# ScalarE works in pairs of steps in the hyperbolic attention loop

## The reference, cut to what matters

```python
q = split_heads(x @ Wq.T); k = split_heads(x @ Wk.T); v = split_heads(x @ Wv.T)
diff_sq = jnp.maximum(q_norm_sq + k_norm_sq - 2.0 * qk, 0.0)
denom = jnp.maximum((1.0 - CURV * q_norm_sq) * (1.0 - CURV * k_norm_sq), 1e-06)
cosh_arg = jnp.maximum(1.0 + 2.0 * CURV * diff_sq / denom, 1.0)
distance = jnp.where(cosh_arg > 1.0, jnp.arccosh(jnp.maximum(cosh_arg, 1.0 + 1e-12)), 0.0)
attn = jax.nn.softmax(-distance, axis=-1)
out = jnp.einsum('bhnm,bhmd->bhnd', attn, v)
```

## Time and profile before

| What | Value |
|---|---|
| median of the runs | 1381.49 us (1377.48 to 1388.93) |
| profiled execution, its own time | 1367.83 us |
| span of that execution | 1365.8 us |
| mean granted TensorE clock | 0.71 of full speed |
| TensorE busy | 974.9 us, 71% |
| VectorE busy | 962.9 us, 71% |
| ScalarE busy | 762.0 us, 56% |
| GpSimd busy | 492.1 us, 36% |

### The profile page before, as it was taken

How to read it: one execution, slowest core, us unless ns; L and a number is a source line. 1 busy time by engine, 2 the same in 40 slices (tenths; PEclk the granted TensorE clock), 3 DMA queues, 4 the chain that set the end, 5 groups by cost and what they waited for, 6 DMA issues and landing times. The chain is left out here.

```text
span 1365.8 us, 17519 instructions
## 1 busy us (share of the span) xinstructions
PE 974.9 (71%) x5593; PEld 495.0 (36%) x5593; DVE 962.9 (71%) x2073; ACT 762.0 (56%) x986; POOL 492.1 (36%) x294
## 2 busy tenths in 40 slices
PE   5887822589999637999364678887787889164385
PEld 2553221256666436998120001111111112034384
DVE  6676598368888263555678999999999999236511
ACT  4204513226666603443243599999999999931031
POOL 0000000200000005664145686888678786200075
PEclk9997965659999957999575555555555555655588
DMA  4001000213110006663234100100010000020064
GB/s 145 0 0 28 0 0 19 68 38 98 42 35 25 9 32 201 214 210 128 75 93 135 44 23 27 41 25 23 24 36 34 24 23 0 0 64 5 36 185 138
DMA packets 59289, 80.25 MB, mean 59 GB/s; under 512 B 13185, under 2 KB 36540, under 8 KB 58944
## 3 DMA queue, kind: packets, MB, share of 16 engines
q1 hardware_dynamic: 50208, 67.33, 15.5%
q0 software_dynamic: 3968, 8.13, 2.0%
q10 hardware_dynamic: 5024, 3.67, 0.8%
HBM read 63.56 MB, written 15.34 MB: 58 GB/s over the span
## 5 line engine op out<-in xcount | busy, mean ns | idle before, releaser
L2483 POOL TENSOR_TENSOR hb_t<-hb_t,hb_r 128x1024 f32<-128x1024 f32 x124 | 330.0, 2699 | 110.1 <-ACT hb_r L2301 110.1
L2238 PE MATMUL hb_psR<-ha_q,ha_k 20*128 20x512 bf16 x256 | 126.3, 592 | 59.8 <-DVE hb_dpos L2495 59.4
L2495 DVE TENSOR_SCALAR hb_dpos<-hb_psR 128x1024 f32<-128x1024 f32 x128 | 155.6, 1217 | 18.9 <-PE hb_psR L2229 10.1
L2503 DVE SCALAR_TENSOR_TENSOR hb_t<-hb_psR,hb_dpos 128x1024 f32<-128x1024 f32 x128 | 155.1, 1212 | 0.0
L2250 PE MATMUL hb_psO<-hb_t,ha_va 128*9 128x512 f32 x512 | 111.5, 969 | 56.2 <-ACT hb_t L2324 56.2
L1843 ACT ACTIVATE ga_att<-ga_psB 128x512 f32<-128x512 f32 (+3 forms) x256 | 102.1, 453 | 74.5 <-PE ga_psB L1775 69.8
L1864 DVE TENSOR_REDUCE ga_nm<-ga_psA 128x1 f32<-128x128 f32 (+3 forms) x256 | 114.3, 485 | 36.0 <-PE ga_psA L1751 32.5
L2229 PE MATMUL hb_psR<-ha_q,ha_k 78*128 78x512 bf16 x256 | 126.2, 595 | 10.0 <-DVE hb_t L2503 3.0
L2512 DVE SCALAR_TENSOR_TENSOR hb_r<-hb_t 128x1024 f32<-128x1024 f32 x64 | 124.5, 1946 | 0.0
L2324 ACT ACTIVATE hb_t<-hb_t 128x4096 f32<-128x4096 f32 x32 | 113.8, 3602 | 0.0
L1625 POOL MEMSET ga_q<- 64x8192 bf16 x1 | 6.9, 6920 | 248.5 <-POOLq L1552 248.5
(11 more groups left out here) (469 smaller groups left out, 2213.5 us busy)
## 6 DMA issues: line engine op xcount, KB each, us to landing
m2x_e_w<-in_L_ffn_W_dram SPq DMA_DIRECT2D x78, 256.0 KB
m1x_e_w<-in_L_ffn_W_dram SPq DMA_DIRECT2D x23, 256.0 KB, 3.2
ga_q<-qx SPq DMA_DIRECT2D x48, 96.0 KB
ha_q<-hqx SPq DMA_DIRECT2D x48, 96.0 KB
ha_k<-hkx SPq DMA_DIRECT2D x16, 288.0 KB
hy_fwd<-in_const_fwd_dram SPq DMA_DIRECT2D x1, 2048.0 KB
f_down<-in_L_ffn_W_dram ACTq DMA_DIRECT2D x4, 512.0 KB, 4.7
hsx<-hp_aparts SPq DMA_DIRECT2D x6, 288.0 KB, 4.3
```

The costliest lines, as they stand in the source:

```text
L2238: mm = pe.matmul(psR[:, side_slot(n), i, :], k[SIDE:SIDE + SROWS, it % 2, i0 + i, P * c:P * c + P], q[SIDE:SIDE + SROWS, it % 2, i0 + i, : ...
L2483: pool.tensor_tensor(tt, tt, r[:, (2 * it + form) % R_QUADS, k, :], ALU.add).then_inc(sum_ready, 1)
L2495: dve.tensor_scalar(dpos[:, n % 2, :], psR[:, dist_slot(n), :, :].rearrange("p i t -> p (i t)"), 0.0, None, ALU.max).then_inc(dpos_ready, 1)
L2503: dve.scalar_tensor_tensor(out=unit(t, n), in0=psR[:, side_slot(n), :, :].rearrange("p i t -> p (i t)"), scalar=CAP, in1=dpos[:, n % 2, :] ...
```

## The change

ScalarE takes the steps in pairs: the roots of both steps of a pair, one change of table, then the logarithms and exponentials of both, without a lag. In the first step of a pair both logarithms stand before both exponentials; in the second each logarithm is followed by its exponential. `copy_batch` stands behind the pair, and the last one behind the loop.

TensorE's calls for the values, and VectorE's copy of a step's output, get their places by the parity of the step, since the weights of an odd step now follow those of the even one closely. The values of an even step stand at n = 8 it + 24 to 27, those of an odd step at 8 it + 21 to 24; the copies at 8 it + 28 and 8 it + 26. Nothing else moves: GpSimd's order, the DMAs, the buffers and the semaphores are the same.

```diff
-            VALUES_AT = (23, 24, 27, 28)
-            COPY_AT, TURN_AT, OUTPUT_AT = 28, 31, 31
+            VALUES_AT = ((24, 25, 26, 27), (21, 22, 23, 24))
+            COPY_AT = (28, 26)
+            TURN_AT, OUTPUT_AT = 31, 31
...
-                            if due(n, VALUES_AT[c]) is not None:
-                                values(due(n, VALUES_AT[c]), c)
+                            for odd in range(2):
+                                it = due(n, VALUES_AT[odd][c])
+                                if it is not None and it % 2 == odd:
+                                    values(it, c)
...
-                    for it in range(STEPS + 3):
-                        if it < STEPS:
+                    for first in range(0, STEPS, 2):
+                        for it in (first, first + 1):
                             product_roots(it)
                             two_roots(it)
-                        if 1 <= it < STEPS + 1:
-                            act.preload_act_table_set("natural_log_exp_and_others")
-                            logs(it - 1, 0)
-                        if it >= 3 and (it - 3) % G == G - 1:
-                            copy_batch((it - 3) // G)
-                        if 1 <= it < STEPS + 1:
-                            logs(it - 1, 1)
-                            weights(it - 1, 0)
-                            weights(it - 1, 1)
+                        act.preload_act_table_set("natural_log_exp_and_others")
+                        logs(first, 0)
+                        logs(first, 1)
+                        weights(first, 0)
+                        weights(first, 1)
+                        logs(first + 1, 0)
+                        weights(first + 1, 0)
+                        logs(first + 1, 1)
+                        weights(first + 1, 1)
+                        if first >= G and first % G == 0:
+                            copy_batch(first // G - 1)
+                    copy_batch(BATCH - 1)
...
-                        if due(n, COPY_AT) is not None:
-                            copy_out(due(n, COPY_AT))
+                        for odd in range(2):
+                            it = due(n, COPY_AT[odd])
+                            if it is not None and it % 2 == odd:
+                                copy_out(it)
```

## The result

The changed kernel takes 1397.73 us (median of four runs, 1396.01 to 1399.15), the kernel before in the same rounds 1380.41: a ratio of 1.0112, with a 95% interval of 1.0087 to 1.0137. It is slower by about 1%, 1.7 us above the range forecast, and at the time that the second rival gave.

The account below looks back on a forecast made before the run. ScalarE was taken to bound the loop, VectorE 7 us behind. Loads -21.0, waits for VectorE -3.7, waits for GpSimd +19.2, ring +0.8 and tail +1.1 gave -3.6: 1378 us, 1372 to 1384; 8 in 10: 1361 to 1396.

Parts of the forecast that it names:

- the second rival: TensorE's odd step and VectorE's even one set the pair, 57.8 to 60.1 us; 1398 us in all; chance 0.2.
- the cover: Even step: VectorE waits for GpSimd anyway, 2 to 4 us a pair, which hides TensorE's longer odd step.
- VALUES_AT, COPY_AT: TensorE: seven value calls in the odd step, one in the even; odd step 29.0 us, 1 to 1.5 over VectorE's share.
- the 55.6: Time of a pair of steps, set by ScalarE waiting for GpSimd's sixteenth sum; 3.2 us more than ScalarE alone needs.
- 15 table loads: ScalarE's loop: 15 of 30 loads go, at 1.40 us each, saving 21.0 us.
- the sixteen sums: GpSimd's sums of a pair run on end, 43.3 us with six products among them.
- a last pair of 51.9: The last pair pays no wait for GpSimd, since its last four sums are VectorE's own.
- the ring's wait of 0.8: Second step's roots wait 0.8 us for the first four sums (three r buffers), hidden except in the last pair.
- the tail's +1.1: TensorE's turning of step 14's output stands behind two value calls awaiting the last exponential: +1.1 us.
- ScalarE's wait for the sum: ScalarE waits about 3 us for the sixteenth sum before a pair's last logarithm, in each of six pairs.
- the six roots' 21.3 us: ScalarE's six roots of a pair: twice 7.03 us and one spacing of 3.61, together 21.3 us.
- The -3.7 of VectorE's waits: ScalarE's 3.7 us of waits for VectorE's product in the loop vanish, swallowed by the longer pair.

Follow-up runs that it names:

- the values spread: Changed kernel with the odd steps' value calls and copy moved into the even step of the loop, four calls per step: 1380.15 us, ratio 0.9960.
- The order alone: ScalarE's new order of pairs, with the value calls and copies at the places of the kernel before: 1383.38 us, ratio 0.9986.
- The calls made cheap: Changed kernel with TensorE's value calls over 256 of the 512 queries, the other half of the output left constant: 1386.21 us, ratio 1.0010.
- The copy between two products: Pairs with the old places of the values, VectorE's output copy moved to unit 6 of every step: 1399.91 us, ratio 1.0116.
- The gap between sums: Changed kernel with the odd steps' copy two units later, and each GpSimd sum waiting by semaphore for the one before: 1386.26 us, ratio 1.0015.
- the first experiment: Changed kernel with VectorE's copy of an odd step's output two units later, at unit 4 of a step: 1399.04 us, ratio 1.0088.
- half sums: Changed kernel with the value calls spread and GpSimd's sums over half the columns, the other half left out: 1355.77 us, ratio 0.9795.
- the best version of the new order: Pairs with the values spread, and ScalarE's last logarithm and exponential of a pair in two halves: 1376.30 us, ratio 0.9945.

## Why the prediction was wrong, point by point

**The step that failed** is the cover in "*VALUES_AT, COPY_AT*": "in the even step VectorE will wait for GpSimd anyway ... some 2 to 4 us a pair". In the changed kernel VectorE's product has no such wait (0.0 in its row below), and with the values spread it is 0.9 us in all, where 2 to 4 a pair were forecast. So the time that TensorE's bunched calls and the copy would cost was put at nothing, and it was there in full: 29.6 us for the even step and 27.7 for the odd one, 57.2 in place of 55.6. I had worked out GpSimd's and ScalarE's time for a pair, but not VectorE's. The earlier trace rows would have shown how near it was: VectorE was busy 352.1 of 363.6 us, and in the stretch of the earlier trace rows this row of before adds 7.3 of waiting for TensorE (its columns are those of the earlier trace rows):

```profile
L2495 DVE TENSOR_SCALAR hb_dpos<-hb_psR 128x1024 f32<-128x1024 f32 x104 | 126.5, 1216 | 11.1 <-PE hb_psR L2229 7.3 <-DVE hb_t L2503 0.5
```

Together that is 98.8%, by which VectorE would need 54.5 of a pair of 55.2 us. That is an upper estimate, since a wait can go when another engine is faster: the kernel before without its loads shows two steps that VectorE bounds at 53.1 to 53.8. So VectorE had room for 1.1 to 2.4 us more a pair before it passed the 55.6 that I forecast, and it took more.

What the bunched calls and the copy did is best seen in VectorE's rows of each kernel, some with ScalarE's first root, 800 to 1215 us (busy time, mean ns, then idle before it and what ended that). After:

```profile
L2501 DVE TENSOR_SCALAR hb_dpos<-hb_psR 128x1024 f32<-128x1024 f32 x103 | 125.6, 1220 | 19.8 <-PE hb_psR L2230 16.0 <-DVE hb_t L2509 0.9
L2518 DVE SCALAR_TENSOR_TENSOR hb_r<-hb_t 128x1024 f32<-128x1024 f32 x52 | 108.0, 2076 | 0.0
L2304 ACT ACTIVATE hb_r<-hb_r 128x4096 f32<-128x4096 f32 x14 | 50.6, 3617 | 35.8 <-DVE hb_r L2518 35.7
```

The values spread:

```profile
L2509 DVE SCALAR_TENSOR_TENSOR hb_t<-hb_psR,hb_dpos 128x1024 f32<-128x1024 f32 x104 | 126.2, 1214 | 3.7 <-PE hb_psO L2251 3.7
L2501 DVE TENSOR_SCALAR hb_dpos<-hb_psR 128x1024 f32<-128x1024 f32 x103 | 125.5, 1219 | 12.1 <-PE hb_psR L2230 8.4 <-DVE hb_t L2509 0.9
L2518 DVE SCALAR_TENSOR_TENSOR hb_r<-hb_t 128x1024 f32<-128x1024 f32 x52 | 90.3, 1736 | 0.9 <-POOL hb_t L2489 0.9
L2304 ACT ACTIVATE hb_r<-hb_r 128x4096 f32<-128x4096 f32 x14 | 50.6, 3611 | 4.5 <-DVE hb_r L2518 4.4
```

The order alone:

```profile
L2501 DVE TENSOR_SCALAR hb_dpos<-hb_psR 128x1024 f32<-128x1024 f32 x103 | 125.4, 1217 | 10.2 <-PE hb_psR L2230 6.0 <-DVE hb_t L2509 0.9
L2518 DVE SCALAR_TENSOR_TENSOR hb_r<-hb_t 128x1024 f32<-128x1024 f32 x52 | 93.5, 1798 | 4.8 <-POOL hb_t L2489 4.8
```

The calls made cheap:

```profile
L2501 DVE TENSOR_SCALAR hb_dpos<-hb_psR 128x1024 f32<-128x1024 f32 x104 | 126.5, 1217 | 5.5 <-DVE hb_t L2509 0.9
L2518 DVE SCALAR_TENSOR_TENSOR hb_r<-hb_t 128x1024 f32<-128x1024 f32 x52 | 112.7, 2167 | 0.0
```

The copy between two products:

```profile
L2501 DVE TENSOR_SCALAR hb_dpos<-hb_psR 128x1024 f32<-128x1024 f32 x105 | 127.9, 1218 | 8.4 <-PE hb_psR L2230 2.6 <-DVE hb_t L2509 0.5
L2518 DVE SCALAR_TENSOR_TENSOR hb_r<-hb_t 128x1024 f32<-128x1024 f32 x54 | 124.3, 2301 | 0.0
```

The gap between sums:

```profile
L2503 DVE TENSOR_SCALAR hb_dpos<-hb_psR 128x1024 f32<-128x1024 f32 x102 | 124.1, 1217 | 14.0 <-PE hb_psR L2230 10.8 <-DVE hb_t L2511 0.9
L2520 DVE SCALAR_TENSOR_TENSOR hb_r<-hb_t 128x1024 f32<-128x1024 f32 x52 | 96.4, 1854 | 0.0
```

Taking the products (52 by their mean) and the waits for TensorE (of both lines) from these rows, and from the same two rows of the first experiment (2.09 us, 15.2) and of before in the stretch of the earlier trace rows, which has 52 products too:

| Kernel | products, us | waits for TensorE, us | sum against after | loop against after |
|---|---|---|---|---|
| after | 108.0 | 16.0 | | |
| before | 102.3 | 7.3 | -14.4 | -14.5 |
| copy later | 108.7 | 15.2 | -0.1 | +1.7 |
| values spread | 90.3 | 12.1 | -21.6 | -20.6 |
| order alone | 93.5 | 6.0 | -24.5 | -18.8 |
| calls cheap | 112.7 | 0 | -11.3 | -11.3 |
| copy between | 119.7 | 2.6 | -1.7 | -0.4 |
| sums apart | 96.4 | 10.8 | -16.8 | -14.2 |

Two lines of VectorE account for the loop within 3 us in each kernel but the one with the order alone; there VectorE also waits 4.8 us for GpSimd's sums, and with these the difference is under 1. The table is a count of VectorE's time, not a proof of what causes it; the causes rest on the experiments. Of the 14.4 us between before and after, 8.7 are waits for TensorE (the seven calls) and 5.7 products that meet sums.

**Rival 2** said this: TensorE's odd step and VectorE's even one, 57.8 to 60.1 a pair, 1398 us. All pairs but one of the six took 57.6 to 59.5, and the time was 1397.7. Its mechanism is the one that the rows show. Its even step is right (29.6, between my 28.8 and 31.1); its odd step was 27.7, not 29.0, and TensorE, busy 27.3 of it, set it. That the time came out so near the middle of this rival is in part luck, since the pairs in which a batch is turned are 1.7 us longer for a reason that it doesn't name. I gave it 0.2 because of the cover that wasn't there.

**Right**: 15 table loads in the loop in place of 30, at nearly the price taken (1.28 us for 1.40, from the pairs of 52.6 with half sums); the sixteen sums of 42 to 43 us; a pair of 55.6 and a last pair of 51.9 where the calls are spread (55.9 and 51.6); the ring's wait of 0.8 (0.94 in the pair shown); the tail's +1.1 (+1.0). ScalarE's wait for the sum, 3 us by the forecast, showed as 1.9: the sum ends where it was forecast, 47.1 us after that pair's first root, but the ring's wait before it had already taken 0.9, and ScalarE's own work 0.2 more than I took. **Wrong besides the cover**: the six roots' 21.3 us hold two spacings of 3.61, not the one that is named; the total is right. The -3.7 of VectorE's waits "which the longer pair swallows" came back as 35.7.

The Trainium skill, page "SBUF — State Buffer", section "Who interferes with whom", says that a VectorE instruction with two inputs in SBUF contends with a GpSimd instruction that reads SBUF, and that the lock on the ports that they share is exclusive. The rows agree: the product reads t twice and takes 1.21 us when it comes first and 3.42 when it comes just after; VectorE's other two operations of a unit, which read PSUM and at most one input in SBUF, stay at 1.21 to 1.22 on average.

What stays open: why the product wins or loses when it and the sum start within 20 ns of each other. With the calls spread it mostly won, from 19 ns before the sum's start to 7 after, but lost at 4, 8 and 17. With the copy later the second product of even steps lost at 8 to 20 ns after, while the fourth product of the steps won at up to 9; in the changed kernel one won at 19. No run here tells what decides.

## What to carry to other kernels

When a change takes time from the bounding engine, add up the next engine's whole period, its waits included, before believing the gain: here VectorE was 1 us a step behind ScalarE, and what it and TensorE lost gave back the whole saving. Where two engines exclude each other, an operation of 0.68 us put between two others can move the next one into the middle of the other engine's instruction, and that cost 1.6 us here (2.82 against 1.21). Moving it out is no cure by itself: in the first experiment the product then came just after the start of a sum and lost 2.2 us. Read the rows again after each such move. A regrouping should be tried first with all else left in place, and only then with each part moved by itself.

## What the runs showed that I had not expected

Where a VectorE product and a GpSimd sum start within 20 ns of each other, the product took 1.21 or 3.42 us, and in one kernel it lost so in every even step from step 2 on; with a gap between sums that kernel's loop was 15.8 us shorter, about 1% of the whole program. The wait that makes the gap costs GpSimd 0.12 us a sum (2.44 us apart in place of 2.32) and made the kernel before faster by 0.46% (0.24 to 0.68), the same as the best version of the new order within the intervals (0.55%, 0.33 to 0.76).
